# A four-stage f32 kernel on one core: rates spread by loads, whole query folds, first norms made ahead, and other column groups

## What is computed

```python
# x: 24 x 128 rows in all (the input padded to a multiple of 8 frames, 8 frames stacked: 2560 values a row)
x = rms_norm(x, ln_pre)                    # over 2560
h = x @ w1.T                               # 2560 -> 1024
h = silu(h[..., 512:]) * h[..., :512]      # gate * value
y = rms_norm(h @ w2.T, ln_post)            # 512 -> 1024
# attention, 32 heads, on z = layernorm(y)
q  = rms_norm(z @ wq_a.T) @ wq_b.T         # 1024 -> 256 -> 32 * (64 + 64)
kv = rms_norm((z @ wkv_a.T)[..., :64]) @ wkv_b.T      # 64 -> 32 * (64 + 128)
h  = y + softmax(mask(q k^T * scale)) v @ wo.T
# last stage, on z = layernorm(h)
base   = z @ base_W.T + base_b             # 1024 -> 1024
probs  = softmax(z @ router_W.T + router_b)           # 15 values
w      = weights of the 8 experts from the 8 largest probs
lora   = ((z @ A.T) * w) @ B * 2           # 1024 -> 8 * 16 -> 1024
out    = h + base + lora
```

## Time and profile before

| | |
|---|---|
| median of 3 runs | 2467.22 us |
| lowest, highest | 2465.22, 2470.27 us |
| the profiled execution, its own time | 2469.25 us |
| its span | 2467.2 us, 46001 instructions |
| mean granted TensorE clock | 0.982 |
| PE busy | 2349.8 us, 95% |
| weight loads (PEld), beside PE | 2050.8 us, 83% |
| DVE busy | 1809.8 us, 73% |
| ACT busy | 1246.0 us, 51% |
| POOL busy | 1219.1 us, 49% |
| data moved | 379.44 MB, mean 154 GB/s |

### The profile page before, as it was taken

One profiled execution on the slowest core, in us unless ns is written; L12 is line 12 of the kernel. 1 busy time (PEld: TensorE's weight loads), 2 busy tenths in 40 slices (PEclk: granted clock), 3 DMA queues, 4 the chain that ended last, 5 costly groups with the idle time before them and its releaser, 6 DMA issues. The chain is left out here.

```text
span 2467.2 us, 46001 instructions
## 1 busy us (share of the span) xinstructions
PE 2349.8 (95%) x14716; PEld 2050.8 (83%) x14716; DVE 1809.8 (73%) x3547; ACT 1246.0 (51%) x3730; POOL 1219.1 (49%) x1011
## 2 busy tenths in 40 slices
PE   8999999988899988999999999899999997999998
PEld 6888888867566668999999999788888886999998
DVE  8996777685466657889888888655777566777775
ACT  5566554442355448999999999823323222111110
POOL 5666676662132336677767776510675653111110
PEclk9999999999999989999999999999999998999999
DMA  7764567677466640111111111296888996122121
GB/s 243 243 225 149 180 211 261 217 244 274 136 204 211 208 147 26 53 56 40 57 48 55 42 55 63 79 326 193 251 242 236 309 271 219 52 69 69 69 68 51
DMA packets 318257, 379.44 MB, mean 154 GB/s; under 512 B 25472, under 2 KB 227712, under 8 KB 317952
## 3 DMA queue, kind: packets, MB, share of 16 engines
q1 hardware_dynamic: 310320, 349.67, 44.8%
q0 software_dynamic: 7184, 25.69, 2.7%
q10 hardware_dynamic: 576, 2.10, 0.3%
HBM read 295.06 MB, written 81.79 MB: 153 GB/s over the span
## 5 line engine op out<-in xcount | busy, mean ns | idle before, releaser
L1556 ACT ACTIVATE attn_prob<-attn_prob,attn_bias 94x94 f32<-94x94 f32 x1024 | 367.2, 363 | 49.0 <-DVE attn_bias L1632 47.7
L671 DVE TENSOR_TENSOR up_t_lo<-early_raw,up_t_hi 128x512 fp32r<-128x512 f32 (+1 forms) x210 | 221.1, 1057 | 122.7 <-ACT up_t_hi L583 121.1
L525 POOL TENSOR_TENSOR early_raw<-early_raw 128x512 f32<-128x512 f32 (+1 forms) x150 | 227.6, 1521 | 143.6 <-DMA early_raw<-x_f 79.4
L1677 POOL TENSOR_TENSOR attn_prob<-attn_prob,attn_share 94x752 f32<-94x752 f32 x128 | 188.3, 1471 | 178.3 <-DVE attn_share L1640 178.3
L1951 DVE TENSOR_TENSOR out_t_lo<-early_raw,out_t_hi 128x512 fp32r<-128x512 f32 x168 | 162.5, 971 | 144.5 <-ACT out_t_hi L1930 144.1
L1916 POOL TENSOR_TENSOR early_raw<-early_raw 128x512 f32<-128x512 f32 x120 | 170.4, 1425 | 194.5 <-DMA early_raw<-o_t 193.9
L583 ACT ACTIVATE up_t_hi<-early_raw 128x512 fp32r<-128x512 f32 (+1 forms) x210 | 130.8, 623 | 262.2 <-POOL early_raw L525 138.3
L745 PE MATMUL up_ps<-up_t_lo,early_s_hi 128*128 128x512 f32 (+1 forms) x616 | 241.9, 393 | 21.2 <-DVE up_t_lo L671 10.8
L1930 ACT ACTIVATE out_t_hi<-early_raw 128x512 fp32r<-128x512 f32 x168 | 105.2, 632 | 300.0 <-POOL early_raw L1916 149.3
L746 PE MATMUL up_ps<-up_t_hi,early_s_lo 128*128 128x512 f32 (+1 forms) x616 | 238.9, 388 | 0.0
L747 PE MATMUL up_ps<-up_t_hi,early_s_hi 128*128 128x512 f32 (+1 forms) x616 | 238.8, 388 | 0.0
(11 more groups left out here) (256 smaller groups left out, 6653.5 us busy)
## 6 DMA issues: line engine op xcount, KB each, us to landing
early_raw<-o_t SPq DMA_DIRECT2D x288, 256.0 KB, 4.9
early_raw<-x_f SPq DMA_DIRECT2D x240, 256.0 KB, 3.7
shared_ring<-w SPq DMA_DIRECT2D x120, 256.0 KB, 3.7
early_raw<-x_f SPq DMA_DIRECT2D x120, 240.0 KB, 4.0
shared_ring<-wvo SPq DMA_DIRECT2D x96, 256.0 KB, 4.9
o_t<-attn_o_t SPq DMA_DIRECT2D x128, 188.0 KB, 1.9
shared_ring<-wo SPq DMA_DIRECT2D x32, 512.0 KB, 6.7
y<-early_raw POOLq DMA_DIRECT2D x24, 512.0 KB, 3.6
```

Of the source, the lines that this page charges most:

```text
L525: nc.gpsimd.tensor_tensor(both[n % 2][:, 0:w], a, b, SEVEN[i].op_b).then_inc(both_done, 1)
L671: nc.vector.tensor_tensor(t_lo[s % NT][:, 0:w], src, t_hi[s % NT][:, 0:w], ALU.subtract).then_inc(lo_done, 1)
L1556: last = nc.scalar.activation(prob[u % NPR][0:SEQ, h, part], prob[u % NPR][0:SEQ, h, part], ACT.Exp, bias=bias[u % 2][0:SEQ, n:n + 1], sca ...
L1677: nc.gpsimd.tensor_tensor(p4, p4, share[u % 2][0:SEQ, :].unsqueeze(2).broadcast_to((SEQ, 8, SEQ)), ALU.mult).then_inc(prob_done, 1)
```

## The change

1. First stage. `diagonal`, the product with ones, ACT's copies, and the three semaphores are gone. At step 154 DVE turns `r` (transpose in blocks of 32), at step 157 SP waits for it and makes four stores of 24 x 32 values, and ahead of steps 159 to 164 one load of 128 x 512 each, which reads the 512 rates into every partition (256 KB in SBUF), after a wait for the four stores. Gates 0, 2 and 4 move to steps 163, 166 and 169, gates 1, 3 and 5 are at 171, 181 and 191, the values at 176, 186, 189, 196 and 199.
2. Second stage. `wk` comes as a block diagonal of both heads (128 x 128 in place of 128 x 64), `fold_q` is one call of two matmuls with 128 rows and 128 columns ahead of block 2, without `fa_made`. DVE's loop gets `at=0`, the place of its head in the instruction fetch blocks.
3. Third stage. The norms of tiles 1 and 0 are made by DVE ahead of steps 148 and 152, into `begun`, and `xn` of tile 0 is written over tile 2 in `k_t`, which is stored before, and loaded again by the last stage once tile 0 is turned.
4. Last stage. PE turns tile 0 from there. The splits of `w` stand between those of tile 0. Groups are 384, 384 and 400, rows of `w` are padded to 1216, and some tiles lie elsewhere in SBUF. For the last tile, PE does group 2 of all eight blocks first, then groups 0 and 1, and puts the LoRA product of the tile before ahead of block 5.

```diff
-        RATE_AT = {group(5, 1): (0, 1), group(5, 2): (2, 3), group(6, 0): (4, 5)}
+        RATE_AT = STAT_AT + KH + 4
-            GATE_FIRST[KH * group(5, pr + 2) + 0] = 2 * pr
-            GATE_FIRST[KH * group(5, pr + 2) + 3] = 2 * pr + 1
-            VALUE[KH * group(5, pr + 2) + 8] = 2 * pr + 1
+            GATE_FIRST[RATE_AT + 9 + 3 * pr] = 2 * pr
+            GATE_FIRST[KH * group(5, pr + 2) + 1] = 2 * pr + 1
+            VALUE[KH * group(5, pr + 2) + 6] = 2 * pr + 1
...
+                if s == RATE_AT + 3:
+                    sp.wait_ge(rate_turned, 1)
+                    for n in range(4):
+                        sp.dma_start(d["rate"][:, n, :], r_t[32 * n:32 * n + TILES, :]).then_inc(rate_stored, 16)
+                if RATE_AT + 5 <= s < RATE_AT + 5 + len(TOKC):
+                    n = s - RATE_AT - 5
+                    sp.wait_ge(rate_stored, 64)
+                    sp.dma_start(ssq[:, RT * n:RT * n + RT],
+                                 d["rate"][4 * n:4 * n + 4].rearrange("t b j -> (t b j)").unsqueeze(0)
+                                 .broadcast_to((P, RT))).then_inc(rate_in[n], 16)
...
-                g = s // KH
-                if g in RATE_AT and kk == 4:
-                    for n, c in enumerate(RATE_AT[g]):
-                        act.wait_ge(rate_made, c + 1)
-                        nc.scalar.activation(ssq[:, RT * c:RT * c + RT], ps[g % 2][2 + n][:],
-                                             ACT.Copy).then_inc(rate_taken, 1)
...
-                if g in RATE_AT and kk == 0:
-                    pe.wait_ge(taken, 4 * (g - 2) + 4)
-                    for n, c in enumerate(RATE_AT[g]):
-                        pe.wait_ge(diag_done, c + 1)
-                        nc.tensor.matmul(ps[g % 2][2 + n][:], ones, sq[c % 2], start=True,
-                                         stop=True).then_inc(rate_made, 1)
...
-                    if kk == 0 and g in RATE_AT and m >= 2:
-                        pe.wait_ge(rate_taken, RATE_AT[g][m - 2] + 1)
...
-            run_steps(dve, TILES, DEPTH, U, step)
+            run_steps(dve, TILES, DEPTH, U, step, at=0)
...
-                rows = slice(64 * h, 64 * h + 64)
                 for c in range(2):
-                    at = P * c + 64 * h
-                    last = nc.tensor.matmul(ps_f[:, at:at + 64], wqn[b][rows, P * c:P * c + P], wk[b][rows, :],
+                    last = nc.tensor.matmul(ps_f[:, P * c:P * c + P], wqn[b][:, P * c:P * c + P], wk[b][:],
                                             start=True, stop=True)
-                last.then_inc(f_made if h == 1 else fa_made, 1)
+                last.then_inc(f_made, 1)
...
+            def norm(t):
+
+                dve.wait_ge(taken, PAIR * FINAL_HIGH + t + 1)
+                link.step(1 - t)
+                moments(nc, link, c_t[t], bn, begun[t])
+                link.fill()
+                if t == 0:
+                    dve.wait_ge(lent_stored, 16)
+                    nc.vector.tensor_scalar(c_t[lent], c_t[0], begun[0][:, 8:9], begun[0][:, 11:12],
+                                            ALU.subtract, ALU.mult)
+
             for s in range(STEPS):
+                if s in (24 * FINAL_LOW + 4, 24 * FINAL_LOW + 8):
+                    norm(1 - (s - 24 * FINAL_LOW - 4) // 4)
...
-CUT = [0, 390, 780, FW]
+CUT = [0, 384, 768, FW]
+ROW = 1216
...
-            for n in range(EARLY):
-                wf.split_hi(act, n)
-
...
                     for c in range(2):
+                        if first(t, 1):
+                            wf.split_hi(act, c)
...
                     for c in range(2):
+                        if first(t, 1) and c == 0:
+                            wf.split_lo(dve, 0)
                         dve.wait_ge(xhi_done, 2 * t + c + 1)
...
+                        if first(t, 1):
+                            for n in ((1,), (2, 3))[c]:
+                                wf.split_lo(dve, n)
...
-                    base(s, range(0, 4))
+                    ending = isinstance(s[0], int) and s[0] == TILES - 1
+                    groups = (0, 1) if ending else (0, 1, 2)
+                    before = 5 if ending else 7
+                    if ending:
+                        base(s, range(KM), (2,))
+                    base(s, range(0, 4), groups)
```

More of the change, by code:

```diff
@@ L1269, in body @@
                     for n in range(4):
-                        if n % 2 == 1 and f is not None and not late:
-                            fold_q(f, n // 2)
+                        if n == 2 and f is not None and not late:
+                            fold_q(f)
                         if first(t, 1):
@@ L2050, in nth, with xn_of @@
             return kb * (U // per) + u // per + 1
+        def xn_of(t, u):
+            return h[2] if first(t, 1) else xn[u % 2]
         @block.sync
@@ L2116, in body @@
                     if first(t, 1):
-                        for n in range(EARLY, KM + 1):
+                        for n in range(2, KM + 1):
                             wf.split_hi(act, n)
@@ L2225, in _, with base @@
         def _(pe):
-            def base(s, blocks):
+            def base(s, blocks, groups=(0, 1, 2)):
                 t, u, kb = s
@@ L2274, in body @@
                 if s is not None:
-                    base(s, range(4, 7))
+                    base(s, range(4, before), groups)
                 if sl is not None:
@@ L2286, in body @@
                 if s is not None:
-                    base(s, range(7, KM))
+                    base(s, range(before, KM), groups)
             run_steps(pe, TILES, DEPTH, U, body)
@@ L2302, in build @@
         h_in = shared.sems("h_in", 3)
+        begun = [x[:, 16 * i:16 * i + 16] for x in (shared.sb("begun", [P, 64]),) for i in range(2)]
         with ExitStack() as early:
@@ L2367 @@
     wkv_b = np.asarray(L0_attn_wkv_b).reshape(PAIRS, 2, NOPE + VD, KR)
+    wk_pair = np.zeros((PAIRS, 2, NOPE, 2, KR), f32)
+    for n in range(2):
+        wk_pair[:, n, :, n] = wkv_b[:, n, :NOPE]
+    wk_pair = wk_pair.reshape(PAIRS, P, 2 * KR)
     wq_rope = wq_b[:, ::-1, NOPE:, :]
@@ L2398 @@
         "wq_rope": wq_rope,
[L2399 removed]
+        "wk": wk_pair,
         "wv": wkv_b[:, :, NOPE:].transpose(0, 2, 1, 3),
```

155 lines of the change are left out of this document (82 added, 73 removed).

## The result

| | before | changed |
|---|---|---|
| median of 4 runs | 2466.22 us | 2437.76 us |
| lowest, highest | 2465.12, 2470.27 | 2434.26, 2439.96 |
| span of the profiled execution | 2467.2 | 2438.3 |
| mean granted clock | 0.982 | 0.982 |

A forecast was written before the change was run, and what follows sets the result against it. PE, busy for 95% of the span, was taken as the bound. Terms of -16.7, -15.5, -9.5, -3.4 and -1.7 sum to -46.8 us: 2422.4 from the profiled 2469.25, 2420.4 by the median, range 2411 to 2432.

The forecast's parts named there:

- The term: First stage: removing the products with ones and the wait for ACT's copy gives -16.7 us, from -12.5 to -18.
- the cover check: First stage, around the removed wait: some 5 to 7 us of DVE's time become free, so PE finds low parts ready.
- The first of the signs of being wrong: First stage: DVE or DMA waits around steps 160 to 185 would show the forecast wrong; no size given.
- the rates' round trip starves the ring: First stage: a wait for input blocks replaces the copy's wait; stage -12, kernel 2425.1 us, chance 0.18.
- Forecast -15.5: Second stage: one fold call saves 12.6 us, earlier waits 2.2, `at=0` 0.7; from -4 to -17.5.
- the lower bound of 0.79: Second stage: a whole query fold costs at least what a half did, 0.79 us, saving 12.6 us over 16 folds.
- The rival by columns: Second stage: the fold is priced by its columns, so only -4 us; kernel 2431.9 us, chance 0.08.
- Forecast +1.3 in the third, and -10.8 behind it: Norms cost the third stage 1.3 us; last stage's start gains 12.3, less 1.5 for slow restart; together -9.5.
- a sign of being wrong: Third stage: a norm that PE waits for ahead of step 150 would show the forecast wrong; no size given.
- Forecast -3.4: Column groups of 384, 384 and 400: less time beside the columns per matmul, -3.4 us, from 0 to -5.5.
- Forecast -1.7: Kernel's end: the last tile's router sums are ready early, shortening the wait for `hw`; -1.7 us, from 0 to -3.
- The slower rival: Attention: DVE's unplaced loop head stands 4.2 us at some six returns, costing 38 us; kernel only 8 us faster, chance 0.02.

## Why the prediction was wrong

**First stage, the failing step.** The term said -16.7; the kernel with the old first stage says that nothing came, within some 2 us. Its arithmetic of what goes away was right: between 443.28 and 473.20 the steps go at PE's own pace, and the 10.34-us wait is gone. The step that failed is the cover check: "some 5 to 7 us, become free, so PE should find its low parts ready". It compared DVE's busy time in one window with what leaves that window. Three things were wrong with it. First, the window was measured with PE standing for 7.9 of its 27.6 us, in step 180 (it ends there, and not at 184). Without that stand the same work has to fit in 8 us less: DVE's 25.76 us busy and POOL's 22.71 were spread over 27.6 us of which PE used 19.71. Second, DVE and POOL aren't independent there. A low part of 1.7 us is one of 0.7 us that stood beside POOL; cutting POOL's sums let PE run at its pace, so the two together are the bound of the last 3.8 us between steps 178 and 188. What they have late, SP's loads have late too. Third, the gates left the window only to take the lead ahead of it. The first of the signs of being wrong, DVE waits around steps 160 to 185, is what came. The rival "the rates' round trip starves the ring" named a price of 4.3 us and a chance of 0.18; it was the right place, and its own mechanism (SP's stand, the bytes) holds for the lead up to step 165, but not for the larger part behind it. In stage lengths of single profiles the way back goes 587.2, 581.5 with the gates and values late, 579.1 with the rates late, 575.0 with the stores late, 572.3 with POOL's sums cut. A part of the first step down is the granted clock, which falls to its lower level behind PE's waits in the changed kernel, for some 10 us in all, and not in the next three. At 575.0 the stage is 14.7 us below the kernel before, and by the ratios that kernel is 11 to 12 us ahead of the one with the old first stage, so most of the term was to be had, by other places for the same work.

**Second stage.** Forecast -15.5, measured -16.9, and -17 for both edits on their own. The total was near by luck, for reasons that weren't given. A whole fold costs 0.46 us, below the lower bound of 0.79, so 16 folds save 17.9 and not 12.6, and the waits ahead of the halves another 2.2. Of these 20 us some 7 came back as waits for `wv_out`, a term that the sum didn't have. `at=0` was priced at 0.7, by the 2.3 us that PE lost at the turns; that was its price before the folds were short, and is no price afterwards. The rival by columns was wrong, and the Trainium skill's cycles ("TensorE: Matmul & The Clock Gate", section "Back-to-back issue gap") don't order these rows either: 128 columns and 128 rows cost less than 64 and 64.

**Third stage and start of the last.** Forecast +1.3 in the third, and -10.8 behind it. Measured: +4.0 between these two profiles, of which the norms' part is the wait ahead of step 148, 2.7 us here (it went with the norms' place; a norm that PE waits for there was a sign of being wrong), and 26.9 us to the third turn instead of 38.2, -11.3. The mis-sized term is the norm: it was taken at 3.64 us and took 6.0, with two of its small steps at 1.1 to 1.2 us each beside POOL, and half a us of standing ahead of another. A row of before showed the same (`xn` at 2.78 beside POOL instead of 0.81), and I used it only where it stood.

**Groups.** Forecast -3.4, by the pace -3.4. That 400 columns pay about what 390 paid beside their columns holds. The Trainium skill's rule for isolated matmuls, columns/2.4 + 2.5 ns (same page and section), by which nothing should have changed, doesn't hold for these rows.

**End.** Forecast -1.7: the wait for `hw` fell by 1.86 us, and the LoRA products restarted less slowly. From the end of the base to the last matmul's end it is 6.1 us instead of 8.8, so 2.7 came.

**The slower rival** did not come: attention takes 678.6 us. But that a stop at a loop's turn can cost more than what PE loses to it today was its idea, and the second stage shows it.

## What to carry to other kernels

A wait of the bound engine is also a rest for those that feed it. Before its length is booked as a gain, follow the lead of the feeders (when a tile is ready against when it is taken) across the place, and ask how long it lasts if the bound engine doesn't stop; where it is near zero at either end, the wait will come back under another name. The second stage has the same on a small scale: 7 of 20 us saved came back as a wait for ACT. Parts that shorten the bound engine's work and parts that remove a feeder's stop are worth little alone and much together, so time them together before dropping either.

## What the runs showed of the hardware

DVE and POOL slow each other down: a 128x512 low part takes 0.68 us on DVE alone and 1.5 to 1.8 beside a sum on POOL, whose 1.29 us become 1.6 to 1.75. Even an instruction on one column is held: a step of the norm's chain took 0.22 us, and 1.22 while POOL worked on 128x512. The two long steps end at 1991.71 and 1993.34, and the two sums on POOL beside them at 1991.71 and 1993.33. A gate (128x2048) took 2.28 us in some places, 3.37 in others. The Trainium skill, page "Trainium Architecture — The Big Picture", section "What this means for kernel authors", says that within SBUF's engine side only DVE and GpSimd share a pair of ports, by an exclusive lock and not a split of the bandwidth. These rows agree with it. By that rule the forecast could have seen from 25.76 + 22.71 us in the window of 27.6 that the two stood in each other's way there. These busy times already hold what one waited for the other, so their sum is no bound.

A fold of two f32 matmuls with 128 rows and 128 columns took 0.46 us between 512-column matmuls, one of two with 64 rows and 64 columns 0.79.

DVE's stop at the turn of its loop took 4.2 to 6.7 us in the kernels without a place for the head. With it, one stop of 2.85 us is left, at 693.5, and none at the later turns. Why it isn't the same length each time was not tried.

PE's granted clock fell to its lower level in its waits of 10.34 us (for 10 us) and 4.72 us (7 us), right behind that of 2.24 us (3 us), and in the 3.87 and 3.60 us in the second stage without a place for the head (7 us each). With stores later, where no wait of PE in steps 178 to 190 is longer than 1.26 us, it didn't fall there.
